# A two-layer gated cross-attention and expert kernel: normalising and adding expert products on GpSimd, products read out of PSUM four at a time and one tile later, top two by the eight largest

## What is computed

```python
gate = softmax(xf @ gate_w)                   # layer 0; layer 1: sigmoid(x @ gate_W) * route_scale
top2 = top_k(gate, 2); w = top2 / sum(top2)
h = gelu(xf @ w1[e] + b1[e])                  # hidden width 512 (layer 0), 64 (layer 1)
y = sum_e w[e] * (h[e] @ w2[e] + b2[e])       # layer 1: plus a shared expert
x = x + tanh(g_ffn[l]) * y
```

## Time and profile before

| | |
|---|---|
| three timed executions | 1083.42, 1087.45, 1087.77 us (median 1087.45) |
| the profiled execution | 1077.48 us, of which the span of its instructions is 1075.7 us |
| busy share of the span | PE 89%, PEld 62%, DVE 72%, ACT 55%, POOL 43% |
| mean granted TensorE clock | 0.968 of full speed |

### The profile page before, as it was taken

One profiled execution on the slowest core, in us unless ns is written; L12 is line 12 of the kernel. 1 busy time (PEld: TensorE's weight loads), 2 busy tenths in 40 slices (PEclk: granted clock), 3 DMA queues, 4 the chain that ended last, 5 costly groups with the idle time before them and its releaser, 6 DMA issues.

```text
span 1075.7 us, 32337 instructions
## 1 busy us (share of the span) xinstructions
PE 960.7 (89%) x13088; PEld 668.4 (62%) x13088; DVE 775.8 (72%) x1691; ACT 591.1 (55%) x1068; POOL 460.5 (43%) x573
## 2 busy tenths in 40 slices
PE   2487899999989999899998989999999999999974
PEld 0154577776767677666776767666666666665653
DVE  3376585886868778686786877888787878787723
ACT  1044546556565555656546565575657565756640
POOL 5353435432334333343435554464646465652000
PEclk9998899999999999999999999999999999999965
DMA  7645652332323323133364756757575767666200
GB/s 176 126 87 132 140 125 67 71 79 67 59 55 83 68 67 81 32 83 68 77 140 70 157 102 120 155 124 153 127 144 110 157 121 152 125 127 103 40 16 3
DMA packets 95216, 107.26 MB, mean 100 GB/s; under 512 B 22394, under 2 KB 86972, under 8 KB 95068
## 3 DMA queue, kind: packets, MB, share of 16 engines
q1 hardware_dynamic: 95068, 105.19, 47.3%
HBM read 35.89 MB, written 0.46 MB: 34 GB/s over the span
## 4 chain that ended last, share of the span: by engine, by line
PE 78%; ACT 8%; DVE 6%; issue 4%; SPq 2%; DMA 1%; POOL 0%; POOLq 0%; DVEq 0%; ACTq 0%
PE pO L975 16%; PE pST L955 15%; PE pMX L991 15%; PE pFH L1116 6%; PE pKV L1033 6%; PE pKV L1040 6%; PE pFY L1090 5%; DVE mx L904 2%; PE pFY L1051 2%; PE pFY L1094 2%; ACT P L641 2%; ACT L641 2%; PE pFY L1057 1%; ACT HR L678 1%; DVE mx L913 1%
## 5 line engine op out<-in xcount | busy, mean ns | idle before, releaser
L641 ACT ACTIVATE P<-pST 125x448 f32<-125x448 f32 x768 | 400.1, 542 | 372.9 <-PE pST L955 365.9
L913 DVE TENSOR_REDUCE mx<-pMX 112x1 f32<-112x500 f32 x384 | 258.7, 674 | 113.7 <-PE pMX L991 109.2
L991 PE MATMUL pMX<-kop,qmax 104*112 104x500 f16 x768 | 291.7, 394 | 42.9 <-DMA qmax<-qlo 22.1
L955 PE MATMUL pST<-qexp,kop 106*128 106x112 f16 (+1 forms) x3072 | 285.6, 216 | 14.4 <-ACT P L641 7.8
L904 DVE TENSOR_REDUCE mx<-pMX 112x1 f32<-112x500 f32 x384 | 256.1, 667 | 49.6 <-PE pMX L991 46.3
L955 PEld LDWEIGHTS pST<-qexp,kop 106*128 106x128 f16 (+1 forms) x3072 | 204.9, 102 | 139.0 <-issue 61.8
L975 PE MATMUL pO<-P,V 125*17 125x112 f32 x6144 | 225.0, 264 | 0.0
L975 PEld LDWEIGHTS pO<-P,V 125*17 125x17 f32 x6144 | 126.2, 97 | 82.9 <-issue 65.7
L551 POOL CAST khi<-kfull 128x500 f16<-128x500 f32 x96 | 58.9, 613 | 240.9 <-ACT kfull L654 240.6
L991 PEld LDWEIGHTS pMX<-kop,qmax 104*112 104x112 f16 x768 | 97.8, 133 | 84.9 <-DMA qmax<-qlo 23.0
L553 POOL TENSOR_TENSOR klo<-kfull,khi 128x500 f16<-128x500 f32 x96 | 109.2, 1137 | 7.7
(11 more groups left out here) (143 smaller groups left out, 1121.9 us busy)
## 6 DMA issues: line engine op xcount, KB each, us to landing
C<-in_ctxT SPq DMA_DIRECT2D x32, 750.0 KB, 6.0
kop<-khi SPq DMA_DIRECT2D x192, 125.0 KB
kop<-maskop SPq DMA_DIRECT2D x48, 437.5 KB
kop<-klo SPq DMA_DIRECT2D x96, 125.0 KB
qexp<-qmax SPq DMA_DIRECT2D x32, 182.0 KB
maskin<-in_mask SPq DMA_DIRECT2D x8, 656.2 KB, 5.9
kop<-maskop SPq DMA_DIRECT2D x2, 1312.5 KB
qmax<-qhi SPq DMA_DIRECT2D x128, 7.0 KB
```

What stands on the lines that cost most here:

```text
L641: nc.scalar.activation(P[0:KP, slot, h * 4 * T:(h + 1) * 4 * T], pST[0:KP, h, 0:4 * T], ACT.Exp, scale=EXP_SCALE).then_inc(exp_done, 1)
L913: nc.vector.tensor_reduce(mx[:, s % 2, m // PAIRS, m % PAIRS:m % PAIRS + 1], pMX[0:T, 1, 0:CW], AX.X, ALU.max).then_inc(max_done, 1)
L955: mm = nc.tensor.matmul(pST[0:cols, h, i * T:(i + 1) * T], kop[0:ROWS, b, p, tile * KP:tile * KP + cols], qexp[0:ROWS, b, p, :, :].rearran ...
L991: nc.tensor.matmul(pMX[0:T, m % 2, 0:CW], qmax[0:SHIFT0, st.s % 2, p, :, :].rearrange("r j q -> r (j q)"), kop[0:SHIFT0, st.s % 2, p, c * ...
```

## The change

- The pairs of products move: y0 and y1 to visits 10 and 11 of the even step, y2 and y3 to visits 1 and 2 of the odd one, yb to visit 4. y0 and y1 share pFY (four experts, 512 columns), y2 and y3 too.
- DVE reads four experts at once, multiplied by their gates, into `ysc` (one instruction after y1, one after y3); POOL adds the eight products in four instructions between mask part 0 and the split of k1; DVE's residual waits for that sum (`ysum_done`), after taking yb out.
- `xnq` and `xnf` are computed by POOL right behind its power -1/2, no longer by DVE.
- The top two come from DVE's eight-largest instruction and a match-and-replace instead of all pairs compared.
- The attention normalisation on POOL works in place; layer 0's softmax is no longer divided by its sum; four tensors fall away; loops' arithmetic is written without helper functions.

```diff
     if has_end(s):
-        uses += [(1, "y3", 1), (3, "yb", 1)]
+        uses += [(1, "y2", 0), (2, "y3", 1), (4, "yb", 1)]
...
     if has_f(s):
-        uses += [(7, "gT", 1)] + [(9 + i, f"y{i}", 1) for i in range(3)]
+        uses += [(7, "gT", 1)] + [(10, "y0", 0), (11, "y1", 1)]
...
+                    link(nc.gpsimd.tensor_tensor(rkq[:, :], rsq[:, :], keep[:, :], ALU.mult))
+                    if s >= 1:
+                        pool.wait_ge(fh_ready, upto(fh_uses, s - 2, "qT"))
+                        apart(pool)
+                    nc.gpsimd.tensor_scalar(xnq[:, :], xg((s + 1) // 2), mvq[:, 0:1], rkq[:, :],
+                                            ALU.subtract, ALU.mult).then_inc(xnq_done, 1)
                 low_part(st, 0)
                 mask_part(st, 0)
+                if has_end(s):
+                    pool.wait_ge(fy_free, upto(fy_uses, s - 1, "y1", True))
+                    apart(pool)
+                    y0, y1 = ysc[:, 0, 0:2, :], ysc[:, 1, 0:2, :]
+                    link(nc.gpsimd.tensor_tensor(y0, y0, ysc[:, 0, 2:4, :], ALU.add))
+                    pool.wait_ge(fy_free, upto(fy_uses, s, "y3", True))
+                    apart(pool)
+                    link(nc.gpsimd.tensor_tensor(y1, y1, ysc[:, 1, 2:4, :], ALU.add))
+                    link(nc.gpsimd.tensor_tensor(y0, y0, y1, ALU.add))
+                    nc.gpsimd.tensor_tensor(acc[:, 1, :], ysc[:, 0, 0, :], ysc[:, 0, 1, :], ALU.add).then_inc(ysum_done, 1)
                 low_part(st, 1)
                 mask_part(st, 1)
...
-                    nc.gpsimd.tensor_tensor(ON0[:, :], OM[:, s % 2, :], rden[:, :], ALU.mult).then_inc(pool_link, 1)
-                    pool.wait_ge(pool_link, st.at(lambda s: pool_links(s) + n))
+                    link(nc.gpsimd.tensor_tensor(OM[:, s % 2, :], OM[:, s % 2, :], rden[:, :], ALU.mult))
                     nc.gpsimd.tensor_tensor(ON[:, :, :, s % 2, :].rearrange("p r j q -> p (r j) q"),
...
                 mask_part(st, 2)
                 low_part(st, 2)
+                if has_a(s):
+                    pool.wait_ge(statf_done, a_count(s) + 1)
+                    apart(pool)
+                    link(nc.gpsimd.tensor_scalar(vef[:, :], mvf[:, 1:2], EPS, None, ALU.add))
+                    link(nc.gpsimd.tensor_tensor(rsf[:, :], vef[:, :], mhalf[:, :], ALU.pow))
+                    if s >= 5:
+                        pool.wait_ge(fy_ready, upto(fy_uses, s - 2, "xT"))
+                        apart(pool)
+                    nc.gpsimd.tensor_scalar(xnf[:, :], XF[:, :], mvf[:, 0:1], rsf[:, :],
+                                            ALU.subtract, ALU.mult).then_inc(xnf_done, 1)
...
                     elif use == "y":
+                        if s >= 5:
+                            dve.wait_ge(xnf_done, a_count(s))
...
                     elif use == "yb":
                         l = layer_of(s - 4)
-                        nc.vector.tensor_tensor(acc[:, 0, :], pFY[0:T, 0:D], acc[:, 1, :], ALU.add).then_inc(fy_free, 1)
+                        nc.vector.scalar_tensor_tensor(out=acc[:, 0, :], in0=pFY[0:T, 0:D], scalar=gains[0:T, 2 + l:3 + l],
+                                                       in1=XF[:, :], op0=ALU.mult, op1=ALU.add).then_inc(fy_free, 1)
                         freed(fy_free, fy_uses, back, use)
-                        nc.vector.scalar_tensor_tensor(out=xg(lambda s: (s - 5) // 2), in0=acc[:, 0, :],
-                                                       scalar=gains[0:T, 2 + l:3 + l], in1=XF[:, :],
+                        dve.wait_ge(ysum_done, end_count(s) + 1)
+                        nc.vector.scalar_tensor_tensor(out=xg((s - 5) // 2), in0=acc[:, 1, :],
+                                                       scalar=gains[0:T, 2 + l:3 + l], in1=acc[:, 0, :],
                                                        op0=ALU.mult, op1=ALU.add).then_inc(x_done, 1)
-                    else:
-                        for j, e in enumerate(experts_of(int(use[1]))):
-                            y = pFY[0:T, j * D:(j + 1) * D]
-                            if e == 0:
-                                ins = nc.vector.tensor_scalar(acc[:, 0, :], y, gate[:, 0:1], None, ALU.mult)
-                            else:
-                                ins = nc.vector.scalar_tensor_tensor(out=acc[:, j, :], in0=y, scalar=gate[:, e:e + 1],
-                                                                     in1=acc[:, 1 - j, :], op0=ALU.mult, op1=ALU.add)
-                            if j:
-                                ins.then_inc(fy_free, 1)
-                                freed(fy_free, fy_uses, back, use)
-                            else:
-                                link(ins)
+                    elif use in ("y1", "y3"):
+                        k = int(use[1]) // 2
+                        nc.vector.tensor_tensor(ysc[:, k, :, :], pFY[0:T, 0:4 * D].rearrange("t (e d) -> t e d", e=4),
+                                                gate[:, 4 * k:4 * k + 4].unsqueeze(2).broadcast_to([T, 4, D]),
+                                                ALU.mult).then_inc(fy_free, 1)
...
+                    p = ge if layer_of(s - 3) == 0 else gp
...
+                        dve.wait_ge(gexp_done, a_count(s))
+                        if layer_of(s - 3) == 1:
                             link(nc.vector.tensor_scalar(g1[:, :], ge[:, :], 1.0, None, ALU.add))
                             link(nc.vector.reciprocal(g2[:, :], g1[:, :]))
                             link(nc.vector.tensor_scalar(gp[:, :], g2[:, :], bc[0:T, RS:RS + 1], None, ALU.mult))
                     if kt == 2:
-                        nc.vector.tensor_tensor(ggt[:, :, :], pj, pe_, ALU.is_gt)
-                        link(nc.vector.tensor_tensor(geq[:, :, :], pj, pe_, ALU.is_equal))
-                        link(nc.vector.tensor_tensor(gel[:, :, :], geq[:, :, :], before_me[:, :, :], ALU.mult))
+                        link(nc.vector.max(out=top[:, :], in_=p[:, :]))
+                        link(nc.vector.tensor_copy(top2[:, 0:2], top[:, 0:2]))
                     if kt == 3:
-                        link(nc.vector.tensor_tensor(grk[:, :, :], gel[:, :, :], ggt[:, :, :], ALU.add))
-                        link(nc.vector.tensor_reduce(rank[:, :], grk[:, :, :], AX.X, ALU.add))
+                        link(nc.vector.match_replace(out=rest[:, :], in_to_replace=top2[:, :], in_values=p[:, :], imm_value=0.0))
                     if kt == 4:
-                        link(nc.vector.scalar_tensor_tensor(out=gsp[:, :], in0=rank[:, :], scalar=1.5, in1=gp[:, :],
-                                                            op0=ALU.is_lt, op1=ALU.mult))
-                        link(nc.vector.tensor_reduce(gden[:, :], gsp[:, :], AX.X, ALU.add))
+                        link(nc.vector.tensor_tensor(gden[:, :], top[:, 0:1], top[:, 1:2], ALU.add))
+                        link(nc.vector.tensor_tensor(gsp[:, :], p[:, :], rest[:, :], ALU.subtract))
                     if kt == 5:
                         link(nc.vector.reciprocal(grd[:, :], gden[:, :]))
                         nc.vector.tensor_scalar(gate[:, 0:NE], gsp[:, :], grd[:, :], None, ALU.mult).then_inc(gate_done, 1)
...
-                    if has_a(s) and kt == 9:
-                        dve.wait_ge(rstdf_done, st.at(lambda s: a_count(s) + 1))
-                        nc.vector.tensor_scalar(xnf[:, :], XF[:, :], mvf[:, 0:1], rsf[:, :],
-                                                ALU.subtract, ALU.mult).then_inc(xnf_done, 1)
...
+                        if s >= 1:
+                            dve.wait_ge(xnq_done, q_count(s))
+                        link(nc.vector.bn_stats(stq[:, :], xg((s + 1) // 2)), alone=True)
...
-                    if has_q(s) and kt == 3:
-                        dve.wait_ge(rstdq_done, st.at(lambda s: q_count(s) + 1))
-                        nc.vector.tensor_scalar(xnq[:, :], xg(lambda s: (s + 1) // 2), mvq[:, 0:1], rkq[:, :],
-                                                ALU.subtract, ALU.mult).then_inc(xnq_done, 1)
...
+                            if l == 1 and i % 2:
+                                pe.wait_ge(fy_ready, upto(fy_uses, s, f"y{i - 1}"))
+                            for e in experts_of(i):
+                                o = pFY[0:T, columns_of(e)]
```

More of the change, by code:

```diff
@@ L165, in experts_of, with columns_of @@
     return e, e + 2
+def columns_of(e):
+    return slice(D * (e % 4), D * (e % 4 + 1))
 def before(uses, s, freed=False):
@@ L190, in links, with pool_links @@
     if has_f(s):
-        n += 9 + (layer_of(s - 3) == 1) + 2
+        n += 6 + 3 * (layer_of(s - 3) == 1)
+    return n
+def pool_links(s):
+    n = 0
+    if has_q(s):
+        n += 3
+    if is_batch(s - 2):
+        n += 1
+    if has_a(s):
+        n += 2
     if has_end(s):
-        n += 2
+        n += 3
     return n
@@ L306, in build @@
         xnfT = sb("xnfT", [128, T])
+        ones = xnfT
         lg = sb("lg", [T, NE])
```

(43 more changed lines are left out.)

51 lines of the change are left out of this document (14 added, 37 removed).

## The result

Changed kernel: median 1168.62 us (1166.77 to 1182.89), kernel before on the same chip 1085.43. Ratio 1.080, 95% interval 1.071 to 1.090: slower, and by more than twice the forecast. 1168.6 lies outside the range of 1102 to 1141. The profiled execution took 1168.26 us; those of both kernels differ by 90.8.

A forecast was written before the change was run, and what follows sets the result against it. It took PE's order as the path, PE being busy 89% of the span. Its terms summed to +38.3 us, which added to the median of 1087.45 gave 1125.7, rounded to 1125; range 1102 to 1141.

The forecast's parts named there:

- y0 out of the hole: At Gelu, y0 no longer fills PE's idle time and is paid in full: +14.4 us layer 0, +4.6 layer 1.
- The clock, layer 0: Behind the longer idle time at Gelu, PE's granted clock falls in most layer-0 groups: 1.1 us each, +7.4 in all.
- The clock, layer 1: Behind about 1.6 us of idling at Gelu, no clock loss: 0, with up to 3 falls of 1.7 in the range.
- POOL's sum as a new wait: At visit 5 of masked odd steps, DVE's residual, then OM and PE's sum, wait for POOL's additions: +11.2 us.
- yb at visit 4: At the start of visit 5, DVE takes yb ahead of OM, delaying PE's sum about 0.4 a group: +2.8 us.
- y3's product: At the start of visit 3, DVE's four-expert product delays PE's first maximum of visit 4: +2.4 us.
- the top two: At visit 2, two DVE operations replace three, shortening PE's wait in even layer-1 steps by 0.45: -2.7 us.
- The end: In the last group, alone at half clock, fewer product waits for DVE and a shorter top two: -1.8 us.
- (b): Rival, more contention: full falls in each layer-0 group, three in layer 1, residual held by POOL: 1140 us, chance 0.10.
- (c): Rival, faster: the lighter DVE removes PE's waits for it: 1067 us, or 1080 if a third went; chance 0.07.
- (d): Rival, no change: gains from the lighter DVE offset a few small waits, only if y0 still filled the hole; chance 0.05.

The follow-up runs named there:

- a_res: Kernel after, with DVE's wait for POOL's sum and the residual moved from the start of visit 5 to behind both score maxima: 1137.4 us, ratio 1.050.
- b_later: Kernel before, with only y0 to y3 moved to visits 10, 11, 1 and 2 and yb to visit 4: 1157.3 us, ratio 1.076.
- d_memset: Kernel after, with y0, y1 at visit 9, y2 10, y3 11, yb 3, POOL's adds earlier, top-two copy replaced by a filler: 1059.9 us, 0.983.
- a_hole: Kernel after, with y0 put back at visit 9, into PE's idle time ahead of the Gelu results: 1108.9 us, ratio 1.025.
- a_both: Kernel after, with y0 back at visit 9 and the residual with its wait behind both maxima of visit 5: 1072.9 us, ratio 0.994.
- a_twice: Kernel after, with y0's products computed a second time at visit 9, in the Gelu hole, the copy unread: 1160.4 us, ratio 1.071.
- c_thin: a_both, with y1's products computed twice, once more at visit 10: 1094.5 us, ratio 1.016 to the kernel before.
- c_wide: a_both, with visit 10's second score-maximum matmul issued 8 extra times in layer-0 groups, 3 in layer 1: 1091.6 us, ratio 1.014 to the kernel before.
- c_hole_wide: Kernel after, with the Gelu hole filled by issuing visit 10's first score-maximum matmul 8 more times in layer 0, 3 in layer 1: 1131.5 us, ratio 1.051.

## Why the prediction was wrong

Side and mechanism of the first step were right, the size was not. By its own terms, over the groups (kernel before in brackets):

- **y0 out of the hole**, 1.80 and 0.6 us a group: idle time in the hole rose by 1.98 in layer 0 (4.31 against 2.33) and 0.80 in layer 1 (1.79 against 0.99). Right.
- **The clock, layer 0**, 1.1 a group: unmasked groups became 4.1 us longer on average, 2.6 of it more idle time of PE and 1.6 more busy time; masked ones 6.8, of it 3.8 idle and 3.0 busy. The matmuls are the same, so the busy time is the clock's. Mis-sized: some 17 us (5 x 1.6 + 3 x 3.0) instead of 7.4, a part of it behind the wait at visit 5.
- **The clock, layer 1, "I take 0, with up to 3 falls of 1.7 in the range"**: this is the step that failed. The clock fell in all six groups, for 92 us in all. In a group with 13.7 us at half clock PE was busy 58.72 us, against 53.15 in such a group of before: 5.6 lost, and with 20.5 us at half clock 8.6. Over six groups (three, two, and one with 10.2 us) that is near 38 us, of the 52 by which the forecast fell short of the profiled execution. 75 of the 92 us at half clock stand behind the hole, the other 17 (five times 3.4) behind the wait at visit 5. Two errors lie in it. I priced a fall as the 3.4 us seen in the earlier trace rows, where falls of 10.2 and 17.1 us were to come. And I took 1.6 us of idling, "as much as in layer 0 now", as safe, although two of eight layer-0 groups had fallen with it.
- **POOL's sum as a new wait**, 1.7 and 0.9: the place and the steps were right, the size was 2.8 and 1.9 a group (OM's wait 3.0 against 0.17, and 2.2 against 0.35), yb's part of some 0.4 among it. xnq took 0.81 on POOL, not 0.5, and the residual 0.57 beside `khi`, not 0.36, a bound that I had left at 0 in the sum. My own terms also add up to 834.6 for the start of `sum` (833.5 + 0.36 + 0.4 + 0.3), not 834.9, so by them the wait is 1.3 us and the term some 8 us, still further off. And behind this wait the clock fell for another 3.4 us, which no step had. a_res gives the price of all of it: 31 us for a term of 11.2.
- **yb at visit 4**, 0.4: b_later's wait for OM is 0.55 longer than before in layer 0 and 0.35 in layer 1. Right.
- **y3's product**, +2.4, and **the top two**, -2.7: PE's wait for maxima in layer 1 went from 1.60 to 1.46 a group and stayed at 0.36 in layer 0. Both nearly nothing: together they gained 0.14 in layer 1, where the top two alone was to gain 0.45; its copy was held beside the cast, and d_memset, without that copy, gained another 0.47.
- **The end**, -1.8: what follows the last of these groups took 2.2 less. Right.

Of the rivals (b) named the right additions, full falls and a held residual, but counted three falls in layer 1 at 1.7. (c) was wrong: PE's waits for maxima stayed, and the lighter DVE gained next to nothing. The condition of (d), that y0 still filled the hole, is met in a_hole and is not enough (1.025); with the wait at visit 5 undone too, a_both lies 0.6% below the kernel before. The rule that the loser of the shared port blocks for the other's whole instruction (the Trainium skill, "SBUF — State Buffer", two separate sides) agrees with the traces: copy and subtraction end with the cast, the residual 0.14 us behind it. The 0.06 us filler, which reads nothing, went beside it unheld.

What stays open: whether a given layer-1 group falls. With the wait of 2.4 us at visit 5 present, a_hole fell behind the hole in five of six and a_twice in all six; without it, a_both and c_thin fell in two of six, c_wide in one, and the kernel before in none, though PE's waits in the hole were the same. How a wait at visit 5 acts on a hole some 40 us later, and why c_hole_wide's longer single wait of 1.15 us brought no fall at all, no run here shows. Nor does one show why the same products behind the same hole stood at half clock for 17.1 us in most groups of b_later and for 10.2 in most of a_res.

## What to carry to other kernels

Before moving work on a saturated engine, ask what it was filling. Here the matmuls in the hole that ACT makes were free; one visit later they were paid in full, and the hole they left halved PE's clock for 3.4 to 17.1 us behind it. Don't price that by the length of the one fall seen: in a_hole and a_twice, which differ only in four matmuls behind the hole, it lasted 3.4 and 10.2 to 17.1 us. Let a result that comes from another engine be waited for behind the work on which the critical engine depends, not ahead of it.
